# Gated graph network on one core: layer weights loaded later, and the last step in quarters

## What is computed

```python
h = x
for i in range(L):                                   # L = 4
    hw = jnp.einsum('bnc,cd->bnd', h, weight[i])
    m = jnp.einsum('bjn,bjd->bnd', adj, hw)
    h = _gru_cell(m, h, w_ih[i], w_hh[i], b_ih[i], b_hh[i])
return _layernorm(x + h * mask[:, :, None], axis=-1)
# _gru_cell: r = sigmoid(xr + hr), z = sigmoid(xz + hz), n = tanh(xn + r*hn), (1-z)*n + z*h
```

## Time and profile before

| | us |
|---|---|
| median of 3 runs | 572.16 (570.96 to 572.51) |
| span of the profiled execution | 570.9 |
| PE busy | 544.4 (95%) |
| PEld busy | 446.3 (78%) |
| DVE busy | 431.5 (76%) |
| ACT busy | 302.0 (53%) |
| POOL busy | 227.1 (40%) |

### The profile page before, as it was taken

The page is one execution under the profiler, slowest core; times in us unless marked ns, Lnnn a source line. Parts: engine busy times, 40 slices in busy tenths (PEclk is TensorE's granted clock), DMA queues, the critical chain, the costliest instruction groups (busy, mean ns, idle before and its releaser), DMA issues.

```text
span 570.9 us, 7455 instructions
## 1 busy us (share of the span) xinstructions
PE 544.4 (95%) x2536; PEld 446.3 (78%) x2536; DVE 431.5 (76%) x726; ACT 302.0 (53%) x454; POOL 227.1 (40%) x156
## 2 busy tenths in 40 slices
PE   5899999999999999999999999999999999999970
PEld 4567888888888888888888888888888888888860
DVE  3998787875778888877667889887577898675475
ACT  3864444447775434545876454445877444444432
POOL 0054334443265444433266443333364633433302
PEclk9999999999999999999999999999999999999995
DMA  7972233002500109401600017701520013000002
GB/s 233 394 240 75 74 111 110 1 0 105 191 1 1 39 22 331 127 0 53 243 0 0 0 37 232 245 0 37 174 84 0 2 37 111 0 1 0 1 1 76
DMA packets 38125, 48.39 MB, mean 85 GB/s; under 512 B 1656, under 2 KB 29904, under 8 KB 38096
## 3 DMA queue, kind: packets, MB, share of 16 engines
q1 hardware_dynamic: 38096, 48.02, 25.3%
HBM read 43.82 MB, written 4.19 MB: 84 GB/s over the span
## 4 chain that ended last, share of the span: by engine, by line
PE 89%; DVE 7%; ACT 1%; issue 1%; DMA 1%; SPq 0%; POOL 0%; DVEq 0%; ACTq 0%
PE p_S L398 38%; PE p_r L408 5%; PE p_r L410 5%; PE p_r L409 5%; PE p_z L408 5%; PE p_z L410 5%; PE p_z L409 5%; PE p_tr L369 5%; PE p_hn L408 2%; PE p_hn L410 2%; PE p_hn L409 2%; PE p_xn L408 2%; PE p_xn L410 2%; PE p_xn L409 2%; DVE low L720 2%; PE p_tr L349 1%
## 5 line engine op out<-in xcount | busy, mean ns | idle before, releaser
L1003 POOL TENSOR_TENSOR work<-hT,work 128x512 f32<-128x512 f32 x62 | 99.1, 1598 | 284.1 <-ACT work L565 283.9
L398 PE MATMUL p_S<-adj_hi,nat_hi 128*128 128x512 f32 x480 | 187.4, 390 | 0.0
L398 PE MATMUL p_S<-adj_hi,nat_lo 128*128 128x512 f32 x480 | 186.9, 389 | 0.0
L398 PEld LDWEIGHTS p_S<-adj_hi,nat_hi 128*128 128x128 f32 x480 | 90.1, 188 | 18.6
L398 PEld LDWEIGHTS p_S<-adj_hi,nat_lo 128*128 128x128 f32 x480 | 90.1, 188 | 18.5
L720 DVE TENSOR_TENSOR low<-low,adj_in 128x1024 int32<-128x1024 int32 x64 | 94.3, 1473 | 0.5
L1007 POOL TENSOR_TENSOR work<-work 128x512 f32<-128x512 f32 x62 | 88.4, 1426 | 4.9
L851 DVE SCALAR_TENSOR_TENSOR work<-p_hn,bias,work 128x512 f32<-128x512 f32 x64 | 47.9, 749 | 55.0 <-ACT work L565 55.0
L565 ACT ACTIVATE work<-p_r,bsum 128x512 f32<-128x512 f32 x64 | 44.1, 689 | 73.5 <-PE p_r L410 73.4
L796 DVE TENSOR_TENSOR hT<-work 128x512 f32<-128x512 f32 x64 | 43.9, 686 | 30.4 <-POOL work L1007 30.0
L565 ACT ACTIVATE work<-p_z,bsum 128x512 f32<-128x512 f32 x64 | 44.1, 689 | 41.0 <-PE p_z L410 41.0
(11 more groups left out here) (130 smaller groups left out, 915.5 us busy)
## 6 DMA issues: line engine op xcount, KB each, us to landing
adj_in<-in_adj_dram SPq DMA_DIRECT2D x64, 512.0 KB, 5.4
x_in<-in_x_dram SPq DMA_DIRECT2D x8, 512.0 KB, 11.2
y<-in_x_dram SPq DMA_DIRECT2D x8, 512.0 KB, 5.0
out_dram<-y SPq DMA_DIRECT2D x7, 512.0 KB, 3.3
out_dram<-y SPq DMA_DIRECT2D x2, 256.0 KB, 3.0
y<-in_L_gnn_w_ih_dram SPq DMA_DIRECT2D x2, 192.0 KB, 3.4
y<-in_L_gnn_w_hh_dram SPq DMA_DIRECT2D x2, 192.0 KB, 4.1
work<-in_L_gnn_w_ih_dram SPq DMA_DIRECT2D x1, 192.0 KB, 2.6
```

Of the source, the lines that this page charges most:

```text
L398: last = nc.tensor.matmul(p_S[h][:, :], part[:, s, j], adj_hi[:, s, j, half(h)], start=(j == 0 and part is nat_hi), stop=(j == NB - 1 and ...
L1003: nc.gpsimd.tensor_tensor(t_sb[:, h], hT[:, s, half(h)], n_sb[:, h], ALU.subtract).then_inc(d_sub, 1)
```

## The change

What it does, part by part:
- SyncE loads layer 0, then graph 0's adjacency, the bias and mask rows, x of graph 1 and layer 1; graph 1's adjacency; layer 2; and, after the second join, layer 3. ScalarE issues the load of x of graph 0 as its first instruction. The loads of y and of graph 2 wait for all four joins instead of all transpositions.
- TensorE transposes layer 0's weights and x of graph 0, and joins. Layer 1 is transposed within the sums of step 1 after block 3 (behind a wait for the low parts of graph 1's transposed x) and joined after block 6; layers 2 and 3 are transposed in steps 2 and 3 after block 1 of the first half and joined after that half. The state products of step 0, half 0, stand between the first three blocks.
- VectorE converts the odd blocks of graph 0 as well, and its copies and splits of the weights follow TensorE's new places.
- The flag is made in step 6 of the last pair, and an engine no longer waits for the normalisation before it reads it; SyncE reads it ahead of its wait for the stores.
- In the last step TensorE does the gates of half 0 before the sums of half 1, and transposes the state of half 0 between the state products and the sums' products of half 1. The last half's gates, new state, transposition, residual and statistics go in quarters (`quarter`, `LAST_BLOCKS`), with the new state as (1-z)*n + z*h, whose z*h is GpSimd's. ScalarE normalises two blocks of graph 6 before the last gates and six after, and issues one of the last three stores.

The core of the diff:

```diff
-            for l in range(L):
-                load_layer(l)
+            load_layer(0)
+            for j in range(NB):
+                sp.dma_start(adj_in[:, j], adj_v[0, j]).then_inc(adj_loaded[j], 16)
...
+            sp.dma_start(x_in[:, 1], x_v[1]).then_inc(x_loaded[1], 16)
+            load_layer(1)
             for j in range(NB):
-                wait_adj(sp, 0, j)
+                wait_adj(sp, 0, j, True)
                 sp.wait_ge(adj_checked, j + 1)
                 sp.dma_start(adj_in[:, j], adj_v[1, j]).then_inc(adj_loaded[j], 16)
+            load_layer(2)
+            sp.wait_ge(start_joined, 2)
+            load_layer(3)
...
             transpose_weights(0)
-            transpose_weights(1)
+            transpose_x(0, 0, True)
             join_weights(0)
...
+                        if s == 0 and j < G:
+                            state_product(p, 0, 0, j, first)
+                        elif s == 1 and j == 3:
+                            pe.wait_ge(xT_done, 4)
+                            transpose_weights(1)
+                        elif s == 1 and j == 6:
+                            join_weights(1)
...
+            def aggregate_half(p, g, h, first=False):
+                l, s = divmod(g, 2)
+                for j in range(NB):
...
+                    if first and g in (2, 3) and (h, j) == (0, 1):
+                        transpose_weights(g)
+                last.then_inc(s_done, 1)
+                if first and g in (2, 3) and h == 0:
+                    join_weights(g)
...
+            def last_step(p):                      # TensorE
+                g = STEPS - 1
+                pe.wait_ge(nat_split, HS_IN * p + 2 * (g - 2) + 2)
+                pe.wait_ge(flag_made, 1)
+                aggregate_half(p, g, 0)
+                transpose_former(p, g, 0, False)
+                gates(p, g, 0, False, lambda: transpose_former(p, g, 1, False))
+                aggregate_half(p, g, 1)
...
+                gates(p, g, 1, False, transpose_half)
+                pe.wait_ge(y_added, 4 * p + 2)
+                for n in range(2):
+                    transpose_last(p, n)
...
+            act.dma_start(x_in[:, 0], x_v[0]).then_inc(x_loaded[0], 16)
...
                 for g in range(STEPS):             # VectorE
...
                     if g:
+                        if first and g == 1:
+                            take_xT(0, 1)
+                            copy_weights(1)
+                            take_odd(1, 7)
+                        elif first and g in (2, 3):
+                            copy_weights(g)
                         new_state(p, g - 1, 1)
...
+            def last_step(p):                      # VectorE, from the last half's gates on
...
+                dve.wait_ge(z_act, HS * p + k + 1)
+                nc.vector.tensor_scalar(r_sb[:, 1], z_sb[:, 1], -1.0, 1.0, ALU.mult, ALU.add).then_inc(z_rest, 1)
+                measure(p, 1, 0)
...
+                last_variance(p, 0)
+                last_residual(p, 0)
+                last_measure(p, 0)
+                last_variance(p, 1)
+                last_residual(p, 1)
+                last_measure(p, 1)
+                last_variance(p, 2)
+                for n in range(3):
+                    last_normalise(n)
```

More of the change, by code:

```diff
@@ L459, in body @@
                     if g == 0 and first:
-                        pe.wait_ge(start_lo, L)
-                        pe.wait_ge(rows_out, 2)
+                        transpose_rows()
                     for h in range(2):
                         transpose_former(p, g, h, first)
-                        gates(p, g, h, first)
+                        if last and g == STEPS - 2 and h == 1:
+                            low_total()
+                        gates(p, g, h, first, begun=(first and g == 0 and h == 0))
             pairs(pe, body)
-            pe.wait_ge(low_red, 1)
-            pe.wait_ge(r_act, HS * PAIRS)
-            nc.tensor.matmul(p_r[0:1, 0:1], lowf[:, 0:1], ones[:, 0:1], start=True, stop=True).then_inc(low_sum, 1)
-            for h in range(2):
-                pe.wait_ge(y_added, 4 * (PAIRS - 1) + h + 1)
-                transpose_h(PAIRS - 1, STEPS - 1, h)
             def graph(b):
@@ L542, in take_adj @@
                 act.wait_ge(adj_loaded[j], 16 * (2 * p + s + 1))
[L543 removed]
+                copy(adj_hi[:, s, j], adj_in[:, j]).then_inc(adj_ready, 2 if first else 1)
             def split_x(p, s, first):
@@ L579, in body @@
                     l, s = divmod(g, 2)
+                    if last and g == STEPS - 1:
+                        last_step(p)
+                        break
                     places = ((),) * 4
@@ L611, in body @@
                     fill(1)
+                    if first and g == 0:
+                        act.wait_ge(rows_out, 2)
                     for h in range(2):
@@ new lines, in last_normalise, with last_variance @@
+            def last_normalise(n):
+                dve.wait_ge(rstd_made, B + n)
+                for j in range(LAST_BLOCKS[n].start, LAST_BLOCKS[n].stop):
+                    last = nc.vector.tensor_scalar(y[:, 1, j], y[:, 1, j], mv[:, 1, j, 0:1], rstd[:, 1, j:j + 1],
+                                                   ALU.subtract, ALU.mult)
+                last.then_inc(y_normed, 1)
+            def last_variance(p, n):
+                blocks = LAST_BLOCKS[n]
+                dve.wait_ge(y_stats, 4 * p + 2 + n + 1)
+                for j in range(blocks.start, blocks.stop):
+                    last = nc.vector.bn_aggr(mv[:, 1, j], stats[:, j])
+                last.then_inc(y_aggr, 1)
+                dve.wait_ge(y_aggr, 2 * p + 1 + n + 1)
+                nc.vector.tensor_scalar(vare[:, 1, blocks], mv[:, 1, blocks, 1], EPS, None, ALU.add).then_inc(var_eps, 1)
@@ new lines, in last_residual @@
+            def last_residual(p, n):
+                bank = (p_tr[1], p_S[0][:, :].rearrange("p (i c) -> p i c", c=C))[n]
+                dve.wait_ge(h_tr, HS * p + 2 * STEPS + n)
+                for i in range(HB // 2):
+                    j = LAST_BLOCKS[1 + n].start + i
+                    last = nc.vector.scalar_tensor_tensor(y[:, 1, j], bank[:, i, :], mask[:, (B - 1) * NB + j:(B - 1) * NB + j + 1],
+                                                          y[:, 1, j], ALU.mult, ALU.add)
+                last.then_inc(y_added, 1)
@@ L840, in body @@
                     s_low(p, g, 1)
+                    if first and g == 0:
+                        check_adj(0, 0, 4)
                     for h in range(2):
@@ L852, in body @@
                                                        r_sb[:, h], ALU.add, ALU.mult).then_inc(t_mul, 1)
-                        if ended and not (last and g == STEPS - 1 and h == 1):
+                        if ended:
                             moments(ended[1], h)
@@ L996, in body @@
                                                     hT_lo[:, s, half(h)].bitcast(F32), ALU.add).then_inc(xT_whole, 1)
-                    for h in range(0 if last and g == STEPS - 1 else 2):
+                    for h in range(1 if last and g == STEPS - 1 else 2):
                         k = 2 * g + h
```

414 lines of the change are left out of this document (249 added, 165 removed).

## The result

The changed kernel takes 578.66 us (median of 4 runs, 577.93 to 580.22); the kernel before takes 572.34 beside it on the same chip. The ratio is 1.0124 (95% interval 1.0106 to 1.0143): slower by 1.2%, where 0.6% was forecast (the two medians alone give 1.1%). The direction was right, but the time lies outside the 574 to 577.5 of the forecast: the rise is 6.3 us and not 3.3.

A forecast was written before the change was run, and what follows sets the result against it. VectorE's queue was taken to bound the head and VectorE's chain the tail, TensorE the stretch between. 570.9 + 0.1 (head) + 3.1 (weight work) + 4.7 (join waits) - 4.6 (tail) = 574.2, by run median 575.5; forecast 574 to 577.5.

The forecast's parts named there:

- end behind the last normalisation: Tail: the last store's landing, drain and end follow the last normalisation by 3.3 us instead of 5.9.
- TensorE's start: Head: layer 0's load shares the DMA engines with x, so TensorE's first work comes at 5.5 instead of 4.78.
- what lies around the span: Whole kernel: the median of the runs is 1.26 us above the profiled execution's span.
- VectorE's low parts of graph 1 end: Head: VectorE starts at 7.35, works a stretch of 32.6 us and reaches this point at 40.0 instead of 45.66.
- The waits at the joins: Steps 2 and 3: TensorE waits 2.35 us in each for VectorE's weight copy behind the adjacency check; 4.7 together.
- The 3.1 of weight work: Steps 2 and 3: layers 2 and 3 each add 1.6 us to TensorE, which never waits there; 3.1 together.
- Rival (a): Steps 2 and 3: VectorE reaches the copies in time, no join waits, step 1 some 1.0 earlier; 569.8 us, chance 0.18.
- (c): Head: TensorE's clock falls in the gap and stays at 1.2 GHz behind the low parts, +3.0; 578.5 us, chance 0.10.
- (d): Tail: TensorE's branch still ends last because the flag is read late, gain 2.0 not 4.6; 578.1 us, chance 0.05.
- The term of 0.8 for a lowered clock: Head: a clock lowered by TensorE's idle gap lengthens the work behind the low parts by 0 to 3, taken as 0.8.
- the prediction's 5.8: Head: TensorE's work between the low parts and step 1's state products, layer 1's weights included, takes 5.8 us.
- landing ... I take 2.2: Tail: the last store of 128 KB lands 2.2 us after issue.

The follow-up runs named there:

- e3: Changed kernel with VectorE's copies of layers 2 and 3 moved ahead of the third adjacency check, behind the first half's new state; 573.93 us, ratio 1.0032.
- e6: Changed kernel with x of graph 0 loaded by SyncE behind layer 0's weights instead of by ScalarE; 581.12 us, ratio 1.0159.
- e7: Changed kernel with 20 filler matmuls on TensorE in its wait ahead of block 2 of graph 1; 578.35 us, ratio 1.0125.
- e5: Changed kernel without TensorE's general path for inexact adjacencies (its flag read and branch); 578.32 us, ratio 1.0108.
- e9: Changed kernel with 9 filler matmuls on TensorE ahead of the join product of layers 2 and 3; 578.22 us, ratio 1.0109.
- e12: e1 without TensorE's general path (its flag read and branch); 568.20 us, ratio 0.9935.
- e14: e1 with every engine reading the flag only behind the last normalisation, SyncE behind its stores' landing; 569.67 us, ratio 0.9957.
- e1: Kernel before with the change's last step, early flag and three last stores, but the old start; 569.63 us, ratio 0.9958.
- e13: e3 with each of the eight checks of graph 0's adjacency cut to 32 of 1024 columns; 569.24 us, ratio 0.9952.
- e11: e1 with all three last stores issued by SyncE, where ScalarE issued the middle one; 569.44 us, ratio 0.9954.
- e4: Kernel before with only the flag made in step 6 and read and branched on early, without quarters; 570.80 us, ratio 0.9983.

## Why the prediction was right and wrong

Forecast 575.5 (574 to 577.5), measured 578.66. The mechanism of the loss was right, and three terms of the sum were too small: the end behind the last normalisation (3.3 for 4.7, by the landing of the last store), TensorE's start (5.5 for 6.68), and the join wait, whose effect on the clock was put at nothing (0.7 on the median). The steps in the prediction's order, with what each adds to the miss of 3.2 us:

| Step | forecast | measured | adds |
|---|---|---|---|
| what lies around the span | 1.26 | 1.8 | +0.55 |
| VectorE's low parts of graph 1 end | 40.0 | 40.80 | +0.8 |
| from there to the state products of step 1 | 6.6 | 6.5 | -0.1 |
| steps 2 and 3 (work and waits) | 7.8 | 7.7 | -0.1 |
| from step 4 to the last step | 0 | -0.3 | -0.3 |
| last normalisation against the shifted one | -2.0 | -1.8 | +0.2 |
| end behind the last normalisation | 3.3 | 4.7 | +1.4 |
| median above the profiled run | 0 | 0.73 | +0.7 |

**Right: the main mechanism.** The waits at the joins were forecast at 2.35 each, behind a check that GpSimd holds, and came at 2.20 and 2.14; e3 shows that they are worth 4.7 of the time. The 3.1 of weight work in steps where TensorE never waits is 2.9 in e3's trace. The shift over steps 2 and 3, 8.5 less 0.77 at the state products, is 7.7 for 7.8 (4.34 of waits, 2.9 of work, the rest behind the waits). Rival (a), copies in time, had its condition wrong for this kernel, but e3 shows what it would have given: 573.9 and not 569.8, since the other 4 us of the start stay. Rivals (c) and (d) had times near the measured one, 578.5 and 578.1, by chance: (c)'s term of 3.0 behind the low parts is at most 0.8 (below), and (d)'s late branch did not happen.

**Wrong in size: TensorE's start.** The step "I take 5.5, with bounds 4.8 and 6.2" failed: 6.68, outside its bounds. The two loads did not share evenly: from 2 to 4 us ScalarE's queue moved 0.49 MB and SyncE's 0.09, x was through by 4.8, and layer 0's weights landed behind it, with the first adjacency blocks in between. The first copy came 1.2 late at 8.53; the stretch of VectorE behind it was right (32.3 for 32.6), so 0.8 was left at the low parts. The Trainium skill (DMA: Bandwidth & Descriptors, section "Issuing engines are not separate DMA queues") had the sign: the trace agrees that a second issuing engine shares the same engines, 6.68 for 4.78. But x behind the weights was no cure (e6).

**Right by luck: the clock.** The term of 0.8 for a lowered clock behind the low parts fits the stretch (6.5 for 6.6), but not for its reason. The granted clock, 0.50 from 36 to 40.6 us, was back soon after the low parts arrived at 40.80. With the full clock all through (e7) the stretch is 6.2 (40.67 to 46.90), and where the clock came back later (e3, e5) it is 7.0. So the clock took 0.3 here, up to 0.8 elsewhere, and the rest is work that the prediction's 5.8 was short of. In e7 the time didn't fall at all. Rival (c) placed the danger in the gap of the start; it was in the join wait of step 2, which the prediction had itself found and not asked what it does to the clock. That is the 0.7 of the last row: e5's profile shows it, and e9 fits.

**Wrong: the end.** The step "landing ... I take 2.2" failed: 3.9. The chain was right (the branch is covered, and rival (d) is excluded: TensorE is through at 571.5 with the end at 576.1), and the edit that was costed at nothing, the moved branch, had a second part that nobody waits for: by the traces its fetch, which falls on the last store. e12 prices it at 1.4 in the time, e5 at 1.0; in their profiles the landing goes from 3.9 to 3.0 and 2.9. The last 0.7 to 0.8, down to the forecast's 2.2, is gone only in e14, where no engine's fetch meets the store; that part is not shown by a run of its own. The rest of the new end, with the quarters, is worth the 2.2 us that e14 shows over the kernel before.

**Wrong: the base.** The profiled execution of the kernel before has a span of 570.9; runs whose spans are given take 1.8 more than their span (570.5 and 572.32, 576.1 and 577.93). By that the execution was one of 572.7 (an estimate), above the median of 572.16, and the 1.26 mixed an offset with a draw.

**Open.** What remains of the start, about 4 us in e3 over e1, has 2.9 in TensorE's weight work and 1.3 ahead of the state products of step 1 (47.85 for 46.53), where VectorE's queue (e13) and, by up to 0.9, the clock come in. Which of its instructions could leave the start without loss was not tried. Of the versions run that compute everything, e1 is the fastest with e11 and e14 (569.4 to 569.7): the new end without the new start beats both kernels, by 0.4% and 1.6%.

## What to carry to other kernels

Work that sits in a wait is free, and moved into a step without waits it is paid in full; worse, each product that it hands to another engine and takes back makes a new wait, whose length is set by the longest instruction ahead of the answer in that engine's queue. So place the answering instruction first (one copy moved over one check, in two steps, won 4.7 us), and before moving a load or a start ask which queue's total length holds the stage, not which of its items comes first. At an end, count what a moved branch does in the background as well as how long it waits.

## What the runs showed of the hardware

- A load of 512 KB issued by ScalarE beside SyncE's 448 KB went ahead of it: 0.49 MB against 0.09 from 2 to 4 us, and SyncE's landed at 6.68 instead of 4.78 (5.10 with x behind them).
- TensorE's branch over the general path takes 3.35 us (e4), 3.59 (e14) to 4.65 (e1, changed kernel), and a store of 128 KB issued just behind it lands in 3.6 to 3.9 us, without the branch in 2.9 to 3.0, and with the branch begun behind the issue in 2.2.
- A gap of 2.2 us on a TensorE that is busy on both sides cost it the full clock in some executions and not in others (granted clock 0.56 in e5 and 1.00 in the changed kernel in the 3 us behind it, and e5 differs only at the end), 1.6 us of time in the two profiles that show it.
- 512 KB of one adjacency block, issued at 39.97, landed 4.4 us later with no other load behind it, where the median of three such loads was 3.3 us.
